# A two-pass expert kernel: 24 units of the first pass run among the last chunks' routing

## The reference, cut to what matters

```python
x = x + gnn(layernorm(x), adj, ...)           # x: 128 x 128 nodes x 128
# feed-forward part, on t = layernorm(x) as 16384 tokens of 128
gate_logits = t @ Wg + bg                     # 8 experts
top_w, top_i = top_k(gate_logits, 2)
top_w = softmax(top_w)
for e in range(8):
    h = gelu(t @ W1[e] + b1[e])               # 128 -> 512, erf form
    out = out + w_dense[:, e:e + 1] * (h @ W2[e] + b2[e])   # 512 -> 128
x = x + out
```

## Time and profile before

| | |
|---|---|
| median of 3 runs | 738.47 us (734.89 to 742.24) |
| the profiled execution's span | 738.4 us |
| TensorE busy | 657.4 us, 89% |
| VectorE, ScalarE, POOL busy | 617.8, 525.4, 500.8 us |
| chain that ended last | PE 58%, ACT 18%, DMA 8%, DVE 6% |

### The profile page before, as it was taken

The page is one execution under the profiler, slowest core; times in us unless marked ns, Lnnn a source line. Parts: engine busy times, 40 slices in busy tenths (PEclk is TensorE's granted clock), DMA queues, the critical chain, the costliest instruction groups (busy, mean ns, idle before and its releaser), DMA issues.

```text
span 738.4 us, 17622 instructions
## 1 busy us (share of the span) xinstructions
PE 657.4 (89%) x4878; PEld 598.6 (81%) x4878; DVE 617.8 (84%) x2056; ACT 525.4 (71%) x1470; POOL 500.8 (68%) x469
## 2 busy tenths in 40 slices
PE   6879888998873979999998999999999999999990
PEld 4646666666562879888998999998999999999990
DVE  4899999999997658777887888887888888888881
ACT  5689999999961646666666767766767767767760
POOL 2652767767767857675776776777777777777773
PEclk9999999899955889999999999999999999999996
DMA  8999994547223567599569655499764444444310
GB/s 296 348 369 275 352 324 152 195 147 313 95 87 109 184 175 249 196 339 320 166 213 356 189 163 156 138 325 378 226 168 120 131 122 121 131 124 119 102 40 29
DMA packets 82040, 148.47 MB, mean 201 GB/s; under 512 B 32247, under 2 KB 36352, under 8 KB 81936
## 3 DMA queue, kind: packets, MB, share of 16 engines
q1 hardware_dynamic: 62576, 100.37, 44.3%
q0 software_dynamic: 18496, 46.70, 17.5%
q10 hardware_dynamic: 864, 0.21, 0.1%
HBM read 92.37 MB, written 57.23 MB: 203 GB/s over the span
## 4 chain that ended last, share of the span: by engine, by line
PE 58%; ACT 18%; DMA 8%; DVE 6%; issue 4%; POOL 3%; SPq 1%; POOLq 0%; ACTq 0%; DVEq 0%
PE bank L1391 8%; PE bank L1403 8%; PE bank L1392 8%; PE bank L1393 8%; PE bank L1408 8%; PE bank L1404 8%; DMA row<-rows 7%; ACT hs L687 5%; ACT row L696 5%; PE bank L1377 4%; ACT t_loop L678 4%; PE bank L1419 4%; ACT t_in L671 3%; POOL rows L591 2%; PE bank L1277 1%
## 5 line engine op out<-in xcount | busy, mean ns | idle before, releaser
L756 ACT ACTIVATE act_f<-bank,b_t 128x256 f32<-128x256 f32 x560 | 220.0, 476 | 7.8 <-PE bank L1393 1.6
L637 POOL DMA_INDIRECT rows<-row,to_row x140 | 167.2, 1194 | 74.0 <-issue 51.9
L634 POOL DMA_INDIRECT out_dram<-row,to_row x140 | 168.0, 1200 | 60.2 <-issue 56.4
L591 POOL DMA_INDIRECT rows<-row,slot_low x128 | 136.4, 1066 | 64.5 <-issue 34.8
L1228 DVE TENSOR_TENSOR act_lo<-act_f,act_hi 128x1024 fp32r<-128x1024 f32 x140 | 171.6, 1225 | 4.8
L746 ACT ACTIVATE in_hi<-bank 128x256 fp32r<-128x256 f32 x140 | 53.9, 385 | 154.9 <-PE bank L1377 154.9
L1223 DVE CAST act_hi<-act_f 128x1024 fp32r<-128x1024 f32 x140 | 97.8, 699 | 69.8 <-ACT act_f L756 69.6
L1391 PE MATMUL bank<-in_hi,w_t 128*128 128x256 f32 x376 | 113.5, 302 | 0.0
L1392 PE MATMUL bank<-in_lo,w_t 128*128 128x256 f32 x376 | 105.5, 281 | 0.0
L1393 PE MATMUL bank<-in_hi,w_t 128*128 128x256 f32 x376 | 105.5, 281 | 0.0
L1403 PE MATMUL bank<-act_hi,w_t 128*128 128x256 f32 x376 | 101.2, 303 | 0.2 <-DVE act_hi L1223 0.2
(11 more groups left out here) (225 smaller groups left out, 1658.9 us busy)
## 6 DMA issues: line engine op xcount, KB each, us to landing
row<-rows SPq DMA_DIRECT2D x140, 260.0 KB, 3.7
w_t<-w_split SPq DMA_DIRECT2D x38, 512.0 KB, 6.7
w_up<-w_split SPq DMA_DIRECT2D x18, 512.0 KB, 7.0
xs<-in_x_dram SPq DMA_DIRECT2D x16, 512.0 KB, 5.0
x_t<-in_x_turned_dram SPq DMA_DIRECT2D x16, 512.0 KB, 6.2
rows<-ends_rep SPq DMA_DIRECT2D x15, 260.0 KB, 7.8
b_t<-in_biases_dram SPq DMA_DIRECT2D x140, 2.5 KB
rows<-row,to_row POOLq DMA_INDIRECT x140, 3.7
```

Of the source, the lines that this page charges most:

```text
L591: pool.indirect_dma_start(out=rows, out_offset=bass.IndirectOffsetOnAxis(ap=slot_low[:, r, b:b + 1], axis=0), in_=row[:, r, b, :], in_offs ...
L634: pool.indirect_dma_start(out=out_rows, out_offset=at, in_=got[:, g, j, P:2 * P], in_offset=None, bounds_check=TOKENS - 1, oob_is_err=Fals ...
L637: pool.indirect_dma_start(out=rows, out_offset=at, in_=got[:, g, j, :], in_offset=None, bounds_check=NROWS - 1, oob_is_err=False).then_inc ...
L756: last = act.activation(act_f[:, s, c, :], ps_h(t, half)[:, i, :], ACT.Gelu, bias=b_t[:, w, c:c + 1])
```

## The change

The counts of the first eight chunks (`KNOWN`) give an early table: for each lower expert the whole tiles that those chunks fill for certain, up to 24 units (`EU`). It is worked out in one turn of the chunk loop (`known_units`, eight steps set between the other work of turn 14) and copied in turn 16 (`s_etab`). The first 24 units take their rows from twelve slots of their own (`early_rows`), in banks that the chunks' routing leaves free, with one bank for the rows, one for the outputs and one each for the two halves of the hidden layer. The routing of chunks 13 to 15, the full table and the skips become `tail(k)`, run behind iteration k of the units on TensorE, ScalarE and VectorE; POOL places the chunks' scatters between units' ones. The table of the other units subtracts the tiles already `used` and begins with the lowest expert again. In units 0 to 15 ScalarE casts the whole high part of the GELU's output, in all later ones the first half, and VectorE the second. The weights of the rows of chunks 13 to 15 come from a tanh on ScalarE and two small instructions on POOL, in place of two sigmoids. Later units use one bank for second layers instead of two. `known_units`, cut:

The diff, cut to its core:

```diff
+    NEEDS = 3 * AHEAD
+    KNOWN = CHUNKS // 2
+    EU, ER = 24, 12
+    WHOLE = 16
     def bank_of_outputs(k):
-        return 5 + 2 * (k + BACK) % 3
+        if k < EU:
+            return 5 if k < EU - 4 else 0
+        return (6, 7, 5)[2 * (k + BACK) % 3]
     def bank_of_rows(k):
-        return 5 + (2 * (k - IN) + 1) % 3
+        return 6 if k < EU else (6, 7, 5)[(2 * (k - IN) + 1) % 3]
...
+        early_rows = sb("early_rows", [P, ER, BLK, ROW])
...
         def ps_h(t, half):
-            return bank[:, (2 * t.index + half) % 3, :].rearrange("p (c m) -> p c m", m=TILE)
+            held = 2 + half if t.index < EU else (2, 3, 1)[(2 * t.index + half) % 3]
         def ps_y(t):
-            return bank[:, 3 + t.slot(2), 0:TILE]
+            return bank[:, 4, 0:TILE]
...
 SP
-            sp.wait_ge(s_tab, 1)
+            sp.wait_ge(s_etab, 1)
...
-                sp.wait_ge(s_row[i], 16 * G * PART // 4)
+                sp.wait_ge(s_row[i], 16 * G * KNOWN // 4)
+            early = entries(early_table, EARLY_AT + 1, 0, AHEAD, MOST)
...
+                    if t.index < EU:
+                        if t.index >= ER:
+                            wait_slot(sp, s_out, 16 * BLK, t.back(ER), 16 * BLK)
...
+            for k in range(ER, EU - AHEAD):
+                unit_in(k, now[i], now[i + 1], now[i + 2], None)
+            sp.wait_ge(s_tab, 1)
+            early = entries(table, PASSES, 0, AHEAD, MOST)
+            now += codes(EU, 2)
+            for i in range(4):
+                sp.wait_ge(s_row_b[i], 16 * G * (CHUNKS - KNOWN) // 4)
...
+            for first in range(EU, UNITS, UT):
+                now = codes(first, UT + 2)
...
 POOL
+            def row_weights(t):
+                pool.wait_ge(s_tanh, t.index - (CHUNKS - 4))
+                pool.tensor_scalar(row[:, r, :, W_AT], turned_margin[:], 0.5, 0.5, ALU.mult, ALU.add).then_inc(s_rw, 1)
+                pool.tensor_scalar(row[:, r, :, W_AT + 1], turned_margin[:], -0.5, 0.5, ALU.mult, ALU.add).then_inc(s_rw, 1)
...
-            for k in range(UNITS):
+            for k in range(2):
+                scatter(unit(k))
+            scatter_rows(chunk(CHUNKS - 3))
+            for k in range(2, 5):
+                scatter(unit(k))
+            scatter_rows(chunk(CHUNKS - 2))
+            for k in range(5, 8):
+                scatter(unit(k))
+            scatter_rows(chunk(CHUNKS - 1))
+            for k in range(8, UNITS):
                 scatter(unit(k))
...
 ScalarE
+            def row_tanh(t):
+                act.activation(turned_margin[:], margin[:], ACT.Tanh, scale=0.5).then_inc(s_tanh, 1)
...
+            def whole_hi(t):
+                wait_turn(act, s_mm2, 1, t, -LATE)
+                wait_turn(act, s_act, 2, t, 2)
+                act.activation(act_hi[:, t.slot(LATE + 1)], act_f[:, t.slot(2)], ACT.Copy).then_inc(s_hall, 1)
+            def half_hi(t):
+                wait_turn(act, s_act, 2, t, 1)
+                act.activation(act_hi[:, t.slot(LATE + 1), 0:FC // 2], act_f[:, t.slot(2), 0:FC // 2], ACT.Copy).then_inc(s_hhi1, 1)
+            def tail(k):
+                if k == 0:
+                    copy_t(chunk(CHUNKS - 2), s_h2t_ps, s_h2t, h2T, s_logit)
+                elif k in (1, 2):
+                    norm2(chunk(CHUNKS - 1), chunk(CHUNKS + 3), range(4 * (k - 1), 4 * k))
+                elif k == 3:
+                    copy_t(chunk(CHUNKS - 1), s_h2t_ps, s_h2t, h2T, s_logit)
+                elif k == 4:
+                    row_tanh(chunk(CHUNKS - 3))
...
+            tile_hi(unit(0))
+            norm2(chunk(CHUNKS - 2), chunk(CHUNKS + 2), range(0, 4))
+            tile_hi(unit(1))
+            norm2(chunk(CHUNKS - 2), chunk(CHUNKS + 2), range(4, G))
+            tile_hi(unit(2))
...
 VectorE (tail(k) at the end of iteration k)
+                if k == 0:
+                    last_norms(chunk(CHUNKS - 1))
+                    place_ranks(chunk(CHUNKS - 4))
+                    place_rows(chunk(CHUNKS - 4))
+                elif k == 1:
+                    last_tops(chunk(CHUNKS - 3))
+                elif k == 2:
+                    last_pairs(chunk(CHUNKS - 3))
+                elif k == 3:
+                    last_counts(chunk(CHUNKS - 3))
+                elif k == 4:
+                    place_ranks(chunk(CHUNKS - 3))
+                    place_rows(chunk(CHUNKS - 3))
+                    last_tops(chunk(CHUNKS - 2))
...
+                elif k == 10:
+                    classes(chunk(CHUNKS - 1))
+                elif k == 11:
+                    bases()
+                elif k == 12:
+                    experts()
+                elif k == 13:
+                    places()
+                elif k == 14:
+                    dve.tensor_copy(table[:], ps_table).then_inc(s_tab, 1)
+                elif k == 15:
+                    skips()
...
+                own(dve.tensor_tensor(tiles[:, 0], cls_i[:, 1, 0], used[:, 1], ALU.subtract))
...
-                hidden_hi(unit(k))
+                if k >= WHOLE:
+                    half_hi(unit(k))
                 hidden_lo(unit(k))
+                tail(k)
...
 TensorE (tail(k) at the end of iteration k)
+                if k == 0:
+                    turned_rows(chunk(CHUNKS - 2))
+                elif k == 2:
+                    logits(chunk(CHUNKS - 2), 0)
+                    logits(chunk(CHUNKS - 2), 1)
+                elif k == 3:
+                    turned_rows(chunk(CHUNKS - 1))
+                elif k == 4:
+                    ranks(chunk(CHUNKS - 3))
+                elif k == 5:
+                    logits(chunk(CHUNKS - 1), 0)
+                    logits(chunk(CHUNKS - 1), 1)
...
             def unit_turned(t):
-                wait_turn(pe, s_done, 1, t, -IN - BACK)
+                if t.index < EU:
+                    wait_turn(pe, s_inlo, 1, t, 0)
+                else:
+                    wait_turn(pe, s_done, 1, t, -IN - BACK)
...
             def unit_back(t):
+                if t.index < EU:
+                    wait_turn(pe, s_done, 1, t, 0)
...
-            pe.wait_ge(s_slot, CHUNKS)
```

More of the change, by code:

```diff
@@ L530, in _ @@
+            for k in range(EU - AHEAD, EU):
+                i = k - ER
+                unit_in(k, now[i], now[i + 1], now[i + 2], early[k + AHEAD - EU])
             needs = None
-            for first in range(0, UNITS, UT):
-                if first > 0:
-                    now = codes(first, UT + 2)
+            for first in range(EU, UNITS, UT):
+                now = codes(first, UT + 2)
                 if first <= NU - AHEAD < first + UT:
-                    early = entries(PASSES + 1, 0, AHEAD, MOST)
-                if first < NU + EARLY[1] - AHEAD and first + UT > NU - AHEAD:
-                    needs = entries(2 * PASSES, 0, EARLY[1], NU + 1, 1)
+                    early = entries(table, PASSES + 1, 0, AHEAD, MOST)
+                if first < NU + NEEDS - AHEAD and first + UT > NU - AHEAD:
+                    needs = entries(table, 2 * PASSES, 0, NEEDS, NU + 1, 1)
@@ L982, in turn @@
                 times_out(4)
+                if t.index == KNOWN + 6:
+                    known_units(5)
                 if norms:
@@ L1161, in _ @@
-            for i in range(2):
-                own(dve.tensor_tensor(at_unit[:, 0, i], begun[:, i], base_row[:], ALU.mult))
-                own(dve.tensor_tensor(at_unit[:, 1, i], begun[:, i], dcnt, ALU.mult))
-            own.sync()
-            first, rows_of, seg, lim, at, start = (unit_at_[:, i] for i in range(6))
-            own(dve.scalar_tensor_tensor(out=change[:], in0=expert[:, 2], scalar=1.0, in1=expert[:, 0], op0=ALU.max, op1=ALU.not_equal))
-            own(dve.tensor_reduce(first, at_unit[:, 0], AX_X, ALU.max))
@@ new lines, in experts @@
+            def experts():
+                own.sync()
+                for i in range(3):
+                    own(dve.tensor_tensor(begun[:, i], base, node_to[:, i].unsqueeze(2).to_broadcast([P, PASSES, E]), ALU.is_le))
+                own.sync()
+                own(dve.tensor_reduce(expert[:], begun[:], AX_X, ALU.add))
+                own(dve.tensor_tensor(from_unit[:], begun[:, 0, 1], base[:, 0], ALU.mult))
+                for i in range(2):
+                    own(dve.tensor_tensor(at_unit[:, 0, i], begun[:, i], far[:, 1], ALU.mult))
+                    own(dve.tensor_tensor(at_unit[:, 1, i], begun[:, i], dcnt, ALU.mult))
+                own.sync()
+                own(dve.tensor_tensor(change[:], expert[:, 2], expert[:, 0], ALU.not_equal))
+                own(dve.tensor_reduce(first, at_unit[:, 0], AX_X, ALU.add))
+                own(dve.tensor_reduce(rows_of, at_unit[:, 1], AX_X, ALU.add))
+                own(dve.tensor_reduce(need[:], from_unit[:], AX_X, ALU.max))
+                own(dve.scalar_tensor_tensor(out=start, in0=expert[:, 0:2], scalar=float(TOKENS),
+                                             in1=start_f[:].unsqueeze(1).to_broadcast([P, 2, PASSES]), op0=ALU.mult, op1=ALU.add))
@@ new lines, in skips @@
```

(29 more changed lines are left out.)

497 lines of the change are left out of this document (288 added, 209 removed).

## The result

| | before | after |
|---|---|---|
| median | 739.15 us (734.89 to 742.24, 8 runs) | 746.68 us (739.48 to 752.36, 8 runs) |
| ratio, 95% interval | | 1.0082 (1.0044 to 1.0119) |
| profiled execution, its span | 738.4 us | 739.48, 737.7 us |
| copy of unit 0, of unit 23, of the last | 249.90, 338.72, 721.22 | 225.82, 328.17, 722.12 |

The ratio leaves out the two slowest of the eight executions of after, which were disturbed (751.31 and 752.36 us); the median of the other six is 745.98 us. The profiled execution is the fastest of the eight, with the highest clock (0.979; the others 0.946 to 0.960).

What follows compares the result with a forecast made beforehand. Bounds: ScalarE and VectorE in the chunks, a serial VectorE chain in the table, TensorE in 140 units. From 738.4 us, 8.7 gained by unit 23 and 10.3 given back behind it: 740.0; own range 732 to 746, whole 727 to 755.

Steps and rivals of the forecast that it cites:

- an early start: First unit no longer waits for the full table; TensorE starts it near 211 instead of 240.91, 30 us earlier.
- two-step chain: Interleaved units: transposing back a unit needs the previous unit's sum through one bank; two units take 7.35 us plus tails.
- a burst of loads: Behind unit 23: 22 new visible expert-weight loads at 0.4 us each, 8.8 us.
- The pace of units 0 to 15: Sixteen interleaved units with tails take 78.6 us, 4.9 each; unit 15's copy at 300.
- half clock as an all-or-nothing case: Rival, chance 0.05: TensorE stays at 1.2 GHz through the interleave; sixteen units take 120 us, time 780.
- Units 16 to 23 at 3.4: Last eight early units, without tails and with the shorter cast: 3.4 us each, 27.2 us; unit 17 changes expert.
- What is given back: Behind unit 23, extra expert changes from sorting twice: weight loads and table reading cost 10.3 us, bounds 5 and 15.
- The reading of table entries: At unit 24, SP reads 18 table entries just ahead of a load: 1.5 us.
- POOL's queue: Rival, chance 0.2: scatters staying at 1.70 us make POOL set the early stage; unit 23's marker at 342, time 752.
- Its bound, 328: POOL's scatters and row loads as second bound: unit 23's rows at 314, its marker at 328.
- Tanh: Rival, chance 0.05: tanh is not in GELU's table; six table loads cost ScalarE 10 us, time 745 to 750.
- the rival had 4.3: Faster rival, chance 0.2: interleaved chain looser, 4.3 us per unit; unit 23 at 321, bursts 8 us, time 729.

Runs made afterwards that it cites:

- second trace: The changed kernel run and profiled once more with no edit; profiled execution 743.99 us, median 746.28 us, ratio 1.013 to the kernel before.
- two banks: Changed kernel with outputs of units 5, 7, 9, 11, 17 and 19 in a second bank; 739.69 us, ratio 1.0028 to the kernel before.
- once the chain is loose: Changed kernel with six units' outputs in a second bank and all casts on VectorE; 744.93 us, ratio 1.0071 to the kernel before.
- once the chain was loosened: Changed kernel with outputs of all odd units 3 to 19 in a second bank; 740.28 us, ratio 1.0022 to the kernel before.
- neither loosening: Changed kernel with six units' outputs in a second bank (1.0028), or with chunk 15's scatters behind unit 11's (1.0045); both together 734.95 us, 0.9962.

## Why the prediction was right

The forecast was 740.0 us, 1.6 above the span of 738.4 from which it starts, with 732 to 746 as its own range and 727 to 755 in all. Measured were 746.68 in the median, just above the forecast's own range and inside the whole one, and 1.0082 in the ratio, whose interval crosses 1%. The mechanism is the one that was written: an early start, a two-step chain that eats most of it, a burst of loads that gives back the rest. The forecast loss of 1.6 us was about a quarter of the measured one. That 740.0 lies beside the first trace's 739.48 is luck, since that is the fastest execution of eight; the second trace's 743.99 is the fairer measure, and the terms below are set beside both.

- The start: unit 0 near 226 by the working (224.5 and 1.5), measured 225.82. The eight steps of known_units had 1.5 us of it. The logits of chunk 13 begin at 206.49 instead of 206.06, but they differ by more from one trace of its versions to the next (204.73 to 210.64), so their cost is not measured.
- The pace of units 0 to 15: 4.9 us; measured 4.70, and 4.96 in the second execution; unit 15's copy forecast near 300, measured 296.38 and 300.25. The chain named is the one that binds: two banks cut its waits from 14.2 to 5.2 us. The working named half clock as an all-or-nothing case at 0.05. It comes in pieces, some 1.5 us after a wait; three of them make the second execution's 4.96 out of 4.70. The sum worked at full clock and had them nowhere; its 4.9 was 0.2 too slow for full clock, and the two errors cancel.
- Units 16 to 23 at 3.4, with the change of expert 30 us in all: measured 31.8 and 30.4. Eight times 3.4 is 27.2, so the working has 2.8 us for unit 17's expert. What took their place is at units 16 and 17 (5.82 and 5.09 us), the wait for rows behind POOL: with chunk 15's scatters moved they take 3.36 and 3.94, loads and all.
- Unit 23's copy at 330, measured 328.17 and 330.60. The gain of 8.7 us was 10.5 and 8.1.
- The casts: 1.03 us forecast, 1.06 measured; a half cast 0.60 forecast, 0.65 measured. The later units' rate is unchanged at 3.26, so ScalarE's slack suffices. With the casts on VectorE the chain is shorter (0.34 us less at unit 1), the whole kernel doesn't mind (744.61), and once the chain is loose it is 5.2 us slower.
- What is given back: 10.3 us forecast, 11.4 and 13.4 measured. This is the term that was too small: unit 23 is on time in the second execution (330.60 by 330), and 3.1 us of its distance to the forecast come behind it. Ahead of unit 69, where all of it was expected, 7.9 and 9.4 are seen, and 22 loads alone cost 6.9 to 8.6 in the kernel before. The reading of table entries was put at 1.5 us and at unit 24 only; 3.4 to 3.9 us more are lost at units 69 to 78, which no step had (below).
- The rivals. POOL's queue did not set the whole early stage, but it had a part in it: TensorE waited 4.0 us for rows at two places. Its bound, 328, lay where it was worked out, 328.62 once the chain was loosened. (The rival for a slow POOL adds 7.4 us behind the last scatter, where the bound itself has 3.7 and 2.7; its 752 is 1 us too high by that.) Tanh brought no table load: each of the kernel's two tables is loaded once in the whole trace. The two-step chain was hardly looser than written (4.70 by 4.9 a unit, where the rival had 4.3). The clock stayed at its upper level from 220 us in the first trace, and dropped in pieces in the second.

## What to carry to other kernels

A sort in two parts doubles the runs of equal keys, so count the reloads with the real inputs before moving work ahead of the full sort: here 24 loads of 512 KB more gave back the 10 us that an earlier start by 24 us had left. Take the suspected cost out of both kernels, not of one: without loads the changed kernel was still 4.8 us the slower. Interleaving fills a gap only at the pace of its longest chain through a shared buffer, so look for the one bank or slot that two iterations share, then for the queue right behind it. Here neither loosening alone beat the kernel before (1.0028 and 1.0045), and both together did, by 0.4% (0.9962). When a kernel spreads by 1 or 2%, profile it twice before explaining its trace.

## What the runs showed of the hardware

- The same wait of TensorE, 2.2 us for the same sum, left the clock at its upper level in one execution and was followed by half clock in the next. The Trainium skill (TensorE: Matmul & The Clock Gate, What's actually happening) says that the chip's watch on TensorE's activity is free-running and that the number of slow matmuls differs from run to run; these two traces agree, with 21 matmuls in one and 11 in the other in the same 2 us.
- Where SP's program reads a block of entries of the unit table into registers, nothing is issued for over 4 us. In SP's queue in the changed kernel, between the rows of one unit and the next load, with no wait to speak of:

```profile
489.99 0.33 SPq L512 DMA_DIRECT2D row<-rows  x1
495.25 0.33 SPq L528 DMA_DIRECT2D w_up<-w_split  x1
```

A gap of the same kind in the kernel before:

```profile
521.23 0.33 SPq L474 DMA_DIRECT2D row<-rows  x1
525.89 0.33 SPq L502 DMA_DIRECT2D b_t<-in_biases_dram  x1
```

Such a gap returns every 16 units where nothing else is waited for, in the changed kernel at 536.39, 588.82 and 640.65 us (4.8 to 4.9 us each), and 16 units are what a block has. Both kernels load 22 layers of weights as the second pass begins, one unit after the other. Before, a block of 16 units begins at 64 and at 80, ahead of that burst and behind it; now they begin at 24, 40, 56 and 72, and the reading falls into it. From the copy of unit 69 to that of 78 it takes 35.68 us instead of 32.32, and 35.7 to 38.1 in every version of the changed kernel that loads; without loads it is 29.3 in both kernels. That this reading causes the loss at units 69 to 78 is argued from the rows; no run moved the blocks, and 1.7 of the 3.4 us also appeared once in the kernel before (34.01, in the run with more loads).
